# Layer statistics of the input moved between the RELU low halves, batches two to six

## The reference

```python
xn = (x - mean(x)) / sqrt(var(x) + 1e-5)              # over the 256 features
q, k, v = (gelu(xn @ W1 + b1) @ W2 + b2 for each)     # 256 -> 256 -> 256
scores = (q @ k.T) / sqrt(256 * 512) * tril(ones)     # 512 x 512, no softmax
s = layernorm(scores @ v) * ln_w + ln_b
h = relu(xn @ Wq1.T + b1)                             # Wq = ternary weights, 256 -> 1024
g = silu(h @ Wq2.T + b2)                              # 1024 -> 256
out = x + s * g
```

## Time and profile before

| what | us |
|---|---|
| median of 3 runs (lowest, highest) | 320.83 (319.23, 322.04) |
| the profiled execution's own time | 320.46 |
| its span in the profile | 318.7 |
| around the span (320.46 - 318.7) | 1.8 |
| busy time in the span: PE, DVE, ACT, POOL | 307.7, 246.6, 220.1, 136.5 |

### The profile page before, as it was taken

The page is one execution under the profiler, slowest core; times in us unless marked ns, Lnnn a source line. Parts: engine busy times, 40 slices in busy tenths (PEclk is TensorE's granted clock), DMA queues, the critical chain, the costliest instruction groups (busy, mean ns, idle before and its releaser), DMA issues.

```text
span 318.7 us, 5664 instructions
## 1 busy us (share of the span) xinstructions
PE 307.7 (97%) x1850; PEld 273.7 (86%) x1850; DVE 246.6 (77%) x544; ACT 220.1 (69%) x416; POOL 136.5 (43%) x105
## 2 busy tenths in 40 slices
PE   7899979999999999999999999999999999999994
PEld 7788879888997899888997889978998889988894
DVE  4589797965979669795879759796697958696687
ACT  3386936959487667858579494886678585794862
POOL 3691733349052570609334390526706093322200
PEclk9999999999999999999999999999999999999999
DMA  7950014520004100050003300041000500010001
GB/s 234 386 172 2 0 68 140 182 76 0 3 1 132 66 0 0 31 167 0 0 0 98 100 0 0 0 135 63 0 0 32 166 0 0 0 66 3 0 3 66
DMA packets 15212, 19.06 MB, mean 60 GB/s; under 512 B 1760, under 2 KB 12512, under 8 KB 15200
## 3 DMA queue, kind: packets, MB, share of 16 engines
q1 hardware_dynamic: 14496, 17.98, 17.1%
q10 hardware_dynamic: 704, 0.93, 0.8%
HBM read 14.69 MB, written 4.22 MB: 59 GB/s over the span
## 4 chain that ended last, share of the span: by engine, by line
PE 49%; DVE 17%; ACT 15%; issue 15%; POOL 2%; DVEq 1%; ACTq 0%; POOLq 0%
PE bank L777 47%; ACT r_hi L436 6%; ACT bank L437 5%; DVE gw L686 2%; DVE gw L701 2%; DVE e L675 2%; DVE x_stats L511 2%; DVE s L652 1%; PE bank L769 1%; DVE g_lo L593 1%; DVE s L649 1%; DVE e L608 1%; POOL o_rstd L343 1%; ACT s_hi L444 1%; DVE s_lo L659 1%
## 5 line engine op out<-in xcount | busy, mean ns | idle before, releaser
L664 DVE TENSOR_TENSOR r_lo<-bank,r_hi 128x512 fp32r<-128x512 f32 x64 | 44.1, 691 | 35.1 <-ACT bank L437 35.1
L436 ACT ACTIVATE r_hi<-bank,col 128x512 fp32r<-128x512 f32 x64 | 46.9, 733 | 24.5 <-PE bank L777 24.5
L437 ACT ACTIVATE bank<-bank,col 128x512 f32<-128x512 f32 x64 | 45.3, 709 | 0.0
L314 POOL TENSOR_TENSOR y<-y,xn 128x512 f32<-128x512 f32 x12 | 20.3, 1694 | 53.5 <-DMA xn<-x_norm_rows 53.5
L343 POOL TENSOR_TENSOR o_rstd<-o_var,neg_half 128x2 f32<-128x2 f32 x16 | 11.3, 704 | 68.5 <-ACT o_var L460 68.5
L777 PE MATMUL bank<-xT_lo,w1q 128*128 128x512 f32 x128 | 39.8, 392 | 0.0
L777 PE MATMUL bank<-xT_hi,w1q 128*128 128x512 f32 x128 | 39.8, 392 | 0.0
L444 ACT CAST s_hi<-s 128x512 fp32r<-128x512 f32 (+3 forms) x32 | 14.7, 461 | 32.7 <-DVE s L652 29.9
L417 ACT ACTIVATE g_hi<-bank,col 128x512 fp32r<-128x512 f32 x48 | 33.6, 699 | 5.1 <-PE bank L777 5.0
L777 PE MATMUL bank<-w2q,r_lo 128*128 128x256 f32 x256 | 35.0, 279 | 1.9 <-issue 1.9
L777 PE MATMUL bank<-w2q,r_hi 128*128 128x256 f32 x256 | 34.4, 277 | 0.0
(11 more groups left out here) (131 smaller groups left out, 704.2 us busy)
## 6 DMA issues: line engine op xcount, KB each, us to landing
out<-x_all SPq DMA_DIRECT2D x15, 256.0 KB, 2.2
x_all<-in_x SPq DMA_DIRECT2D x7, 512.0 KB, 3.6
y<-in_x_t SPq DMA_DIRECT2D x6, 512.0 KB, 3.7
xn<-x_norm_rows SPq DMA_DIRECT2D x6, 512.0 KB, 3.5
x_all<-in_w1t SPq DMA_DIRECT2D x1, 1024.0 KB, 10.1
x_all<-in_w2t SPq DMA_DIRECT2D x1, 1024.0 KB, 12.2
row<-in_rows ACTq DMA_DIRECT2D x1, 512.0 KB, 8.0
x_all<-in_x SPq DMA_DIRECT2D x1, 256.0 KB, 3.2
```

Of the source, the lines that this page charges most:

```text
L314: nc.gpsimd.tensor_tensor(half, half, x_mean_all, ALU.subtract).then_inc(xT_centred, 1)
L436: nc.scalar.activation(r["hi"][:, f], pre[:], ACT.Relu, bias=b1)
L437: nc.scalar.activation(pre[:], pre[:], ACT.Relu, bias=b1).then_inc(f1_whole, 1)
L664: nc.vector.tensor_tensor(r["lo"][:, f], bank[(AT_F1 + f) % BANKS][:], r["hi"][:, f].bitcast(FP32), ALU.subtract).then_inc(r_split, 1)
```

## The change

In the loop's batches (i = 1 to 5) the statistics of batch i + 2 are taken apart: the waits and the first `bn_stats` stand behind `r_lo(0)`, the other three behind `r_lo(1)`, `r_lo(2)`, `r_lo(3)`, and the six small instructions behind `r_lo(4)`. Batch 0 keeps them at the old place, batches 6 and 7 have none.

```diff
+            def x_tile_statistics(b, t):
+                nc.vector.bn_stats(x_stats[:, t], x_all[:, b, t]).then_inc(x_stats_made, 1)
+
+            def x_moments(b):
+                aggregate(x_stats, x_part, x_mean, x_var, x_stats_made, STEPS * (b - 1) + TT, x_var_made)
...
                 for t in range(TT):
-                    nc.vector.bn_stats(x_stats[:, t], x_all[:, b, t]).then_inc(x_stats_made, 1)
-                aggregate(x_stats, x_part, x_mean, x_var, x_stats_made, STEPS * (b - 1) + TT, x_var_made)
+                    x_tile_statistics(b, t)
+                x_moments(b)
...
+                inside = not (first or second_last or last)
                 for f in range(FT):
                     r_lo(f)
+                    if inside and f == 0:
+                        dve.wait_ge(x_loaded, 16 * (i + 2))
+                        dve.wait_ge(x_norm_stored, 16 * i)
+                    if inside and f < TT:
+                        x_tile_statistics(i + 2, f)
+                    if inside and f == TT:
+                        x_moments(i + 2)
...
-                    if not second_last:
+                    if first:
                         x_statistics(i + 2)
                     o_scale(0)
```

## The result

The changed kernel takes 325.08 us (median of 6 runs, 322.71 to 326.66) against 320.84 us before (319.23 to 322.08): ratio 1.0138, 95% interval 1.0096 to 1.018, that is 4.2 us slower. Ratios and intervals are estimated from all comparable runs of both kernels and need not equal the quotient of the two medians. Forecast were 323.8 us and a range of 317.7 to 326.4. The result is beyond the 1% line (the interval reaches down to 0.96%), on the side to which I gave 0.40 and not the 0.54 of "within 1%".

What follows compares the result with a forecast made beforehand. PE was taken as the bound, busy 97% of the span. Removing its z waits gives -2.75 us, the new stall +5.7, together +2.95 on the median of 320.83: 323.8 us, range 317.7 to 326.4.

Steps and rivals of the forecast that it cites:

- the old wait: PE idles for DVE's g_lo(1) at z of batches 2 to 6; all five waits go, -2.75 us.
- Four bn_stats for nothing: Between the r_lo, paced by ACT, the bn_stats fit into DVE's idle: cost 0, bounds 0 and 0.05 x 4 per batch.
- The small instructions stand under v_lo: Behind r_lo(4), POOL's v_lo holds DVE's small instructions; PE stalls before the last layer, +5.7 us in all.
- slow first matmuls: PE's first pair after some of the waits is slow, 0.10 us each at most: 0.2 us in the sum.
- Which instruction stands: In batch 1, L495, L496 and L497 go through after v_hi; L500 waits until v_lo ends.
- the comparison with the medians: +2.95 us added to the median of 320.83, 0.37 above the profiled execution, gives 323.8 us.
- Rival 1: At aggregate behind r_lo(4), four-element operands are not held up; the gain alone, 318.1 us; chance 0.25.
- Rival 2: POOL gets in ahead of L495 or L496, all six follow v_lo: +2.0, 325.8 us; chance 0.14.
- Rival 3: The z wait stays, g_lo(1) still late, and the new stall comes on top: 326.5 us; chance 0.03.

Runs made afterwards that it cites:

- moments_old: Changed kernel with only the six small instructions back at their old place ahead of o_scale(0); 319.37 us against 320.69, ratio 0.9925.
- changed_again: The changed kernel once more, unaltered, in five rounds and with a second profile; 325.9 us against 321.83, ratio 1.0135.
- moments_last: Changed kernel with the six small instructions behind r_lo(7) instead of r_lo(4); 318.16 us against 320.69, ratio 0.9909.
- after_o_scale: Kernel before the change with the whole of x_statistics(i + 2) behind o_scale(0) instead of ahead of it; 318.02 us against 322.12, ratio 0.9861.
- four probes: moments_old plus one unused 128x4 instruction behind r_lo(5), differing in kind and input; one run each: 320.77, 321.77, 318.07 and 319.65 us.
- pool_v_first: Changed kernel with POOL's v_hi and v_lo ahead of its four steps on the transposed input; one run, 342.58 us against 321.83.

## Why the prediction was right, and where it was off

**PE is the bound and the old wait is all there is to gain: right.** The waits at z are gone in every kernel in which DVE was relieved ahead of `o_scale(0)`. They cost 2.55 us in all, 2.75 was forecast (36.62 us for a batch without a wait, where it is 36.65). At the end of batch 3 `finish` ends 3.26 us ahead of z (172.01, 175.27), 0.69 earlier than before, where 0.72 was put.

**Four bn_stats for nothing: right**, by `moments_old` and by their 0.42 us in the timeline, with GpSimd busy beside each of the twenty. The row it rested on was weaker than I read it: POOL was busy only up to 13.05 of the 1.40 us that began at 12.39.

**The small instructions stand under v_lo: right in mechanism, off in size.** For batch 1 I worked out 0.9 us, for the others 1.15. From z to the last ternary layer it is 80.29 - 61.98 = 18.31 us in batch 1 and 18.50, 18.29, 18.69 and 18.35 in batches 2 to 5. Against 17.29, which this distance is in `moments_old`, the stalls are 1.02, 1.21, 1.00, 1.40 and 1.06: 5.69, where the forecast had 5.5 and, with 0.2 for slow first matmuls, the term 5.7. That the four later stalls have the forecast mean, 1.17 us against 1.15, is in part luck: POOL's first step came 5.00 us after z in the mean, not 5.14, and from the end of `v_lo` to PE's last layer it took 2.3 us, not 2.09. The five batches lose 6.08 against their unhindered length, and 6.47 in the second profile (stalls by the same count 5.85). The 0.4 more in the first lies behind the stall, where the sum had 0.2. Of it 0.26 is in batch 4: there five groups of eight matmuls of the last layer, behind the first, follow each other at 0.94 us instead of 0.91, with the granted clock at 1.00. The second profile has the same in batches 4 and 5. No row says why; the cause is open.

**Which instruction stands: wrong in detail.** I had L499 pass and L500 wait. L499 waits itself (four batches of five), since a product of one SBUF input with a constant is held too; in batch 3 it is L497, and in the second profile L496 once. That changed the sum little, for any of them ends with `v_lo`.

**The step that was short** is the comparison with the medians. I had +2.95; the two profiles show +3.53 and +3.92 in the six batches, the medians +4.2 and +4.1. Of the 1.3 us that separate forecast and result, 0.6 lie in the first profile's batches (a smaller old wait 0.2, the loss behind the stalls 0.4), and the second profile has 0.4 more, 0.16 of it in longer stalls and the rest again behind them. What is left is not assigned: before z of batch 1 the runs differ by up to 3.1 us (61.98 here, 65.12 in `moments_last`, 63.36 before), and I let one execution stand for that. A part of this spread goes with PE's clock: between 40 and 50 us 0.83 was granted in the profiles of `moments_old`, `moments_last`, `after_o_scale` and `changed_again`, whose z of batch 1 comes at 64.77 to 65.12, and 1.00 before the change and in the first profile after it. So I put the centre a hair under the 1% line, and the chances with it.

**The rivals.** Rival 1 (small operands pass) fell with the four probes. Rival 2 (all six behind `v_lo`) did not come about; L495 got through in all ten batches of the two profiles and L496 in nine. Rival 3 (the z wait stays) fell with the first profile.

## What to carry to other kernels

Before a small instruction is put into a gap of VectorE, look at what GpSimd runs at that moment. In these runs not the size of the instruction counted but its kind and where its inputs lie, and a held one cost the remainder of GpSimd's instruction. `bn_stats`, a reduction, a product from PSUM and a subtraction with one input in PSUM kept their length beside GpSimd; two inputs in SBUF, or a product with a constant from SBUF, did not, and such instructions belong where GpSimd is idle. And a late engine need not be a full one: here the same work one step later, behind the instruction that another engine waits for, gave the whole gain (ratio 0.986, 36.65 us a batch) with a single moved call.

## What the runs showed that I had not expected

- A product of 128x4 elements with a constant, from SBUF, took 1.35 to 2.20 us under `v_lo`, and 0.15 from PSUM.
- After a wait of PE of 2.5 us the granted clock was at 0.50 (1.2 GHz) for nearly 7 us in batch 1 and 3.4 us in each of the others; the waits of 0.8 to 1.3 us in the changed kernel left it at 1.00 in every batch. `pool_v_first` lost 243.12 - 219.90 = 23.2 us in its six batches for some 13.5 us of waiting.
- Three places for the same work (`moments_old`, `moments_last`, `after_o_scale`) give the same batch to 0.01 us; their medians differ by more (319.37, 318.16, 318.02), so they can't be told apart by these runs.
